# Four mixing layers on one core: the token layer's steps placed in adjoining half slots of the sampling stage, the aggregation of windows from half slot 16 in place of 20

## What is computed

```python
x = x + _L0_conv_ref(_gn(x), ...)   # whitening by a covariance over all samples: a 128x128 matrix
x = x + _L1_conv_ref(_gn(x), ...)   # sampling layer: 9 taps a pixel at learned offsets, with a softmax mask
x = x + _L2_conv_ref(_gn(x), ...)   # window attention and, over it, attention among windows
x = x + _L3_conv_ref(_gn(x), ...)   # masked input, ReLU, 3x3 convolution
```

```python
normed = (wtok - mu) / jnp.sqrt(var + LN_EPS) * ln_w + ln_b
g = jax.nn.gelu(normed, approximate=False)
qk = jnp.einsum('oc,bcn->bon', w_qk, gf) + b_qk[None, :, None]
w_dots = jnp.einsum('bhid,bhjd->bhij', w_q * scale, w_k)
w_attn = jax.nn.softmax(w_dots, axis=-1)
agg = jnp.einsum('bhij,bhjnd->bhind', w_attn, wfm)
return jnp.einsum('oc,bchw->bohw', w_out, fmap) + b_out[None, :, None, None]
```

## Time and profile before

| | before |
|---|---|
| median of 3 runs | 9431.34 us (9422.09 to 9446.05) |
| profiled execution | 9447.01 us, span 9445.1 us |
| TensorE matmul busy | 7953.1 us (84%) |
| VectorE busy | 7424.2 us (79%) |
| ScalarE busy | 4160.5 us (44%) |
| DMA queues | 14.1% of 16 engines |
| chain that ended last | PE 49%, DVE 30%, issue 14%, ACT 5% |
| mean granted TensorE clock | 0.923 |

### The profile page before, as it was taken

One profiled execution on the slowest core, in us unless ns is written; L12 is line 12 of the kernel. 1 busy time (PEld: TensorE's weight loads), 2 busy tenths in 40 slices (PEclk: granted clock), 3 DMA queues, 4 the chain that ended last, 5 costly groups with the idle time before them and its releaser, 6 DMA issues.

```text
span 9445.1 us, 289882 instructions
## 1 busy us (share of the span) xinstructions
PE 7953.1 (84%) x123582; PEld 4488.4 (48%) x123582; DVE 7424.2 (79%) x9217; ACT 4160.5 (44%) x7020; POOL 191.3 (2%) x253
## 2 busy tenths in 40 slices
PE   6457898888988888898889889888988988898897
PEld 6324445454444545444454544445454444545454
DVE  2478787978888797888889788888979888897973
ACT  0034535444453544445354544545454444535432
POOL 0000000000000000000000000000000000000000
PEclk7579899999999999899999989999998999999998
DMA  5000111111011111102111110201111120111101
GB/s 120 0 20 17 50 37 43 42 44 49 25 53 33 52 33 45 47 26 56 31 51 33 46 46 27 59 28 50 33 48 44 31 59 25 48 33 48 45 26 56
DMA packets 231852, 391.63 MB, mean 41 GB/s; under 512 B 26736, under 2 KB 168016, under 8 KB 223312
## 3 DMA queue, kind: packets, MB, share of 16 engines
q1 hardware_dynamic: 230544, 372.67, 14.1%
HBM read 190.38 MB, written 130.55 MB: 34 GB/s over the span
## 4 chain that ended last, share of the span: by engine, by line
PE 49%; DVE 30%; issue 14%; ACT 5%; DVEq 1%; DMA 0%; SPq 0%; POOL 0%; ACTq 0%; POOLq 0%
PE ps L765 7%; PE ps L900 7%; DVE arena L1731 6%; PE ps L699 4%; DVE arena L1708 4%; DVE arena L1714 4%; PE ps L1001 4%; PE ps L798 4%; PE ps L991 3%; PE ps L814 3%; PE ps L773 3%; DVE arena L1786 3%; PE ps L787 2%; PE ps L721 2%; DVE arena L1826 2%
## 5 line engine op out<-in xcount | busy, mean ns | idle before, releaser
L900 PE MATMUL ps<-arena,ident 64*64 64x512 f32 x5600 | 1665.9, 646 | 346.3 <-DVE arena L1731 341.7
L902 PE MATMUL ps<-arena,ident 48*64 48x512 f32 x5600 | 1670.8, 647 | 0.0
L1731 DVE TENSOR_TENSOR arena<-arena 112x2560 f32<-112x2560 f32 x560 | 1578.3, 2819 | 7.4 <-PE ps L902 1.4
L900 PEld LDWEIGHTS ps<-arena,ident 64*64 64x64 f32 x5600 | 470.7, 141 | 1314.7 <-issue 1305.7
L765 PE MATMUL ps<-arena,wqk 128*128 128x400 f32 x2048 | 893.8, 554 | 147.5 <-DVE arena L1835 105.8
L699 PE MATMUL ps<-vp,convw 128*128 128x448 f32 x2016 | 832.9, 551 | 19.2 <-ACT vp L1327 19.2
L1714 DVE TENSOR_TENSOR arena<-arena 112x576 f32<-112x576 f32 x1008 | 764.1, 758 | 34.9
L814 PE MATMUL ps<-arena 64*64 64x33 f32 x32768 | 642.2, 226 | 140.3 <-issue 84.1
L1820 DVE COPY arena<-ps 128x400 f32<-128x400 f32 x512 | 293.2, 573 | 539.9 <-PE ps L765 539.6
L1243 ACT ACTIVATE arena<-ps 112x864 f32<-112x864 f32 x224 | 199.2, 889 | 1137.2 <-PE ps L721 1132.4
L1826 DVE TENSOR_REDUCE arena<-ps 128x16 f32<-128x800 f32 x512 | 505.4, 987 | 242.3 <-PE ps L787 238.3
(11 more groups left out here) (300 smaller groups left out, 12693.2 us busy)
## 6 DMA issues: line engine op xcount, KB each, us to landing
windows_out<-arena SPq DMA_DIRECT2D x1024, 100.0 KB
arena<-windows_out SPq DMA_DIRECT2D x224, 256.0 KB, 4.0
arena<-windows_out SPq DMA_DIRECT2D x224, 192.0 KB, 3.3
arena<-in_wqk SPq DMA_DIRECT2D x16, 2048.0 KB, 8.1
arena<-in_x_t SPq DMA_DIRECT2D x16, 1568.0 KB, 10.4
arena<-in_x SPq DMA_DIRECT2D x16, 1568.0 KB, 7.3
arena<-arena SPq DMA_DIRECT2D x32, 784.0 KB
out_x<-xb SPq DMA_DIRECT2D x112, 224.0 KB, 2.0
```

The lines of the kernel that those rows point to most:

```text
L900: nc.tensor.matmul(ps[half, 3, :], ident[0:SLOT, 0:SLOT], prod[0:SLOT, ring(c, dy), dx, :], start=(s < 2), stop=(s >= TAPS - 2), skip_grou ...
L902: mm = nc.tensor.matmul(ps[half, 4, :], ident[SLOT:PT, SLOT:], prod[SLOT:PT, ring(c, dy), dx, :], start=(s < 2), stop=(s >= TAPS - 2), ski ...
L1731: V.tensor_tensor(prod[0:PT, ring(c, dy), :, :].rearrange("p k (n e) -> p k n e", e=CG), taps.to_broadcast([PT, SHIFTS, N64, CG]), for_tap ...
```

## The change

All steps of the chain from the second half of the queries and keys on come earlier: that half at q 9 in place of 10, scores at 11 (12), softmax at 12 (15), its division at 14 (18), transposes at 14 (18), the first group at 16 (20), the group norm at 33 (37). Masks follow four half slots earlier than before; the convolution's pieces begin at 34 in place of 38, keep that distance up to the ninth, and then are spread, so that the last but one stands at 62 in place of 64 and the last where it was, at 68. No instruction is added, dropped or resized.

```diff
-TOK_Q, TURN_Q, Q2_Q, S2_Q, SOFT_Q, A2_Q, AGG_Q = 2, 6, (8, 10), 12, 15, 18, 20
+TOK_Q, TURN_Q, Q2_Q, S2_Q, SOFT_Q, A2_Q, AGG_Q = 2, 6, (8, 9), 11, 12, 14, 16
 GN_Q = AGG_Q + 17
-CONV_Q = [38, 38, 39, 40, 41, 42, 43, 44, 45, 47, 49, 50, 51, 53, 54, 56, 58, 60, 62, 64, 2 * TR * SHIFTS - 2]
+CONV_Q = [34, 34, 35, 36, 37, 38, 39, 40, 41, 43, 45, 47, 49, 51, 52, 54, 56, 58, 60, 62, 2 * TR * SHIFTS - 2]
 ADD_Q = [at + 4 for at in CONV_Q[2:-1:3]] + [2 * TR * SHIFTS - 1]
-MASK_Q = [GN_Q, GN_Q, 39, 40, 42, 44, 47]
-MASKED_Q = [38, 38, 40, 42, 44, 47, 50]
+MASK_Q = [GN_Q, GN_Q, 35, 36, 38, 40, 43]
+MASKED_Q = [34, 34, 36, 38, 40, 43, 46]
@@
-                elif q == SOFT_Q + 3:
+                elif q == SOFT_Q + 2:
                     dve.wait_ge(s2_e.sem, s2_e.at(i))
```

## The result

| | before | after |
|---|---|---|
| median | 9446.05 us (5 runs, 9422.09 to 9475.21) | 9515.8 us (5 runs, 9497.69 to 9547.98) |
| profiled execution | 9447.01 us, span 9445.1 us | 9497.69 us, span 9495.7 us |
| mean granted TensorE clock | 0.923 | 0.924 |

The changed kernel takes 1.0078 times as long, with an interval of 1.0059 to 1.0096: 0.8% slower, where no difference was forecast, and above the range. The profiled execution is the fastest of the five and lies 50.7 us above the one of before, where the medians differ by 70.

The account below looks back on a forecast made before the run. VectorE was taken to set the pace, its waits being what can be moved. Waits at L1928, L1683 and L1973 of 14.6 us against 14.1 a sample, times 15 some 9 us, on the median 9431.3 gave 9440 us, range 9404 to 9474.

Parts of the forecast that it names:

- The early half: Second half of keys, scores and softmax, before slot 8: no new wait, with 0.4 us in hand at scores and exponential.
- The pauses: In the aggregation, odd groups wait for ScalarE's copy of the even one: 1.28 us, or 1.99 where offsets are copied first.
- I carry 3.3 over: In the aggregation, the 3.3 us a sample by which L1928's traced wait (9.8) exceeded the count (6.5) stays.
- L1928's term: VectorE's wait for project_windows in the aggregation: 10.5 us a sample, 0.7 more than before the change.
- the sum: VectorE's waits at L1928, L1683 and L1973 together: 14.6 us a sample against 14.1, so 0.5 to 0.6 more.
- The tail: Group norm, masks and convolution: a new 3.0 us mask wait, L1683 down to 0.5, no convolution piece stopping VectorE.
- L1973's new wait: In slot 18, VectorE waits for ScalarE's third mask: 3.0 us a sample more, with a table load at 1.30.
- At the tightest 0.1 in hand: In the convolution, slots 23 and 24, TensorE follows closely enough that VectorE never waits, with 0.1 us to spare.
- L1973 alone would be worth 44 us: If the new wait for the third mask in slot 18 did not come, that alone would be worth 44 us.
- TensorE's lag decides twice: Rival, chance 0.20: more half-clock stretches in the aggregation make project_windows late; 9489 us with two, 9465 with one.

Follow-up runs that it names:

- before, copy ahead: The kernel before, with ScalarE's copy of the even group put ahead of its copy of the offsets in slot 14: 9396 us, ratio 0.9954.
- after, copy ahead: The changed kernel, with ScalarE's copy of the even group put ahead of its copy of the offsets in slots 9 and 14: 9450 us, ratio 1.0013.
- after, slot 7 filled: The changed kernel, with three products nobody reads put into TensorE's idle time in slot 7 and none in the pauses: 9553 us, ratio 1.0115.
- after, start held: The changed kernel, with its first group held until VectorE's multiplication of slot 9 is done: 9563 us, ratio 1.0142.
- one empty slot: The kernel before with early half drawn together, group pairs in slots 9 to 11 and 13 to 16, and two ScalarE reorderings (even group's copy, masks' exponential): 9359 us.
- the same from 8: The kernel with one empty slot, all seven pairs one slot earlier (8 to 11 and 13 to 15), nothing else changed: 9444 us, ratio 0.9990.
- the filled kernel of 9484 us: The changed kernel, with products nobody reads put into TensorE's idle time in slot 7 and the pauses between groups: 9484 us, ratio 1.0043.

## Why the prediction was wrong

The account of TensorE's aggregation, in us a sample. Pauses and stops are the rows of the waits; half-clock time is twice the length times what the granted clock lacks to 1, summed over the fifteen stretches; the rest is the length less pauses, stops and half of the half-clock time.

| kernel | first group in slot | length | pauses | stops | half clock | rest | L1928 | median |
|---|---|---|---|---|---|---|---|---|
| before | 10 | 80.0 | 4.6 | 0.9 | 4.6 | 72.2 | 9.8 | 9446 |
| after | 8 | 88.1 | 7.8 | 2.3 | 9.6 | 73.2 | 13.5 | 9516 |
| before, copy ahead | 10 | 76.5 | 2.6 | 0.8 | 1.6 | 72.4 | 7.1 | 9396 |
| after, copy ahead | 8 | 82.9 | 3.8 | 2.4 | 6.4 | 73.6 | 10.9 | 9450 |
| after, slot 7 filled | 8 | 91.7 | 7.8 | 3.7 | 14.8 | 72.8 | 16.3 | 9553 |
| after, start held | 8 | 89.9 | 7.8 | 2.2 | 17.4 | 71.2 | 17.5 | 9563 |
| one empty slot | 9 | 82.3 | 1.3 | 0.6 | 3.1 | 79.0 | 4.6 | 9359 |
| the same from 8 | 8 | 86.6 | 2.5 | 2.2 | 7.3 | 78.3 | 7.8 | 9444 |

Within an order the rest moves by 0.2 (from slot 10), by 2.4 (from slot 8, the held start being lowest) and by 0.7 (one empty slot), where the length moves by 3.5, 8.8 and 4.3: most of the account closes. Now the prediction's steps.

**The early half: right.** By the medians slot 6 lasts 10.18 us and slot 7 4.83; L1913 waits in 3 samples, 2.1 us together; no load is waited for.

**The pauses: right.** 7.8 us of them were in the count, 7.76 came.

**"I carry 3.3 over": this step failed.** The excess of stops and half clock was taken as a property of the aggregation that moves with it unchanged. In TensorE's time it was 0.9 + 4.6 / 2 = 3.2 before, and is 2.3 + 9.6 / 2 = 7.1 after; the rest is 1.0 longer, and the first group starts at slot 8 + 6.6 in the mean and not at 5.7. So the seventh project_windows ends at 94.6 from slot 8, where 85.5 was counted and VectorE was to ask at 87.6. VectorE's waits show where it is lost: L1928 in slots 12 to 14 has 9.4 (counted 6.9), and slot 11, where 1.7 us were in hand, has 3.6. The disturbance comes early, in slots 8 to 11, and slot 11's add pays for it. L1928's term was 10.5 and measured 13.5; that is 3.0 of the 4.6 that the sum missed. (The count itself was a little high: its own times, 40.8, 51.1 and 61.0 against 39.6, 49.2 and 57.5, give 6.6 and not 6.9.)

That an excess needn't carry over could have been seen from the order. Before, the first two pairs stand in slots of dy 0 and 1, whose turn and output lie between even and odd group; the pauses come in a TensorE that is already behind and full. After, they stand in dy 3 and 4: the pauses of 1.28 and 1.99 fall into the first ten microseconds, behind slots in which TensorE idles between sums.

**The tail: one right, one small miss.** L1973's new wait was 3.0, measured 2.8, with a table load at the 1.30 of the earlier trace rows in it. The Trainium skill, ScalarE: Activation LUTs, What ACT_TABLE_LOAD costs, adds a drain of about 1.38 us to such a load; by it the wait would have been 4.4, an estimate. The trace disagrees, with 2.8. L1683 was to fall to 0.5 and is at 0.9. "At the tightest 0.1 in hand" in slots 23 and 24 is 0.9 short in slot 23, and the group norm waits 0.4 more at L1560: 1.3 us that were not in the sum. But that L1973 alone would be worth 44 us was wrong: twice, its wait taken away, nothing was gained, since TensorE was behind it.

**The rival that came.** It was "TensorE's lag decides twice", with its sign: a wait at L1928 in slot 16 (0.3 us a sample) and a clock of 0.87 to 0.98 in the aggregation of fourteen samples. It was priced at 9489, and had counted half clock alone; the stops of issue, 1.4 us a sample more, had no place in it. It was given 0.20 against 0.55, although the prediction knew of one undisturbed stretch in fifteen, and the new order had more gaps ahead of it. After the result: one of fifteen samples is undisturbed again, at 272.9 us, what the forecast had for all of them (273.0 + 0.6). The Trainium skill, TensorE: Matmul & The Clock Gate, A second HAM failure mode, says that frequent small idle gaps of TensorE between groups of products make the clock swing between its two levels. The trace agrees: a stop of 1.01 us and a pause of 1.23 stand ahead of the half clock at 1714.05.

**Open.** The stops are waits for packets of instructions, and a stop sits at a fixed place in TensorE's stream (108, 107, 101 products as instructions are put in ahead); 16 of them over 0.2 us fall into slot 9 in fifteen samples of the change, none before. Filling idleness made them more, holding the start did not remove them. Why a packet is asked for so late that it lands behind its need is not shown, and no run changed how the packets come or laid their ends clear of the groups. That a run of 128 products in 1.57 us, 256 instructions with the loads, uses up a packet faster than the next one comes (1.27 us and then 1.40 in the sample above) fits all of this, and is only argued. Nor is it shown how the loss divides between stops and pauses themselves and the half clock behind them, other than by the table's arithmetic: filling raised the clock and gained 32 of 70 us.

## What to carry over

A disturbance that a trace shows as an excess over the count is not a constant to be moved along: say which gaps make it, and look for these gaps in the new order. Where an engine falls behind, the runs here speak for putting dense groups of small products where other work of the same engine covers the hand-over between them; here one exchange in ScalarE's queue was worth 43 to 61 us, one slot's difference in the start 74 to 85. When a trace calls a stop "issue", look at the packets of instructions before calling it causeless. And before a wait is taken away, ask who is late behind it: the mask's 2.8 us a sample, taken away in two ways, and the softmax's 3.2 gave nothing.

## What the hardware showed

- TensorE stood still for 0.2 to 2.5 us (4.0 in the filled kernel of 9484 us) inside runs of 64x64 products and in the sums behind them, at fixed places in its instructions; in the traces of before and after all 83 such stops of the sampling parts end 1.25 to 1.76 us after a 16 KB packet of instructions has landed.
- Half clock of very different length: 17.1 us at 1.2 GHz where 2.30 us of idleness, a stop of 1.89 and a pause of 1.23 stood close together; 3.4 or 6.8 us where 2.9 us of idleness had dense work behind them, and in the kernel of 9359 us project_windows then ran at 2.4 GHz.
- Products that nobody reads, put into idle time, made the kernel slower by 37 us where they only brought the first group forward, and faster by 32 where they also filled the pauses behind it.
